# Preln attention and FFN kernel: the first head's keys by matmul instead of by copies, tables sent earlier, two V batches moved

## The chip, the cores and the metric

One core of one Trainium2 chip runs the kernel. The metric is the device time of one execution in microseconds (us). Of that, the profile shows the span, from the first to the last instruction. Engines are named as in the profile: PE is TensorE's matmul, PEld its weight load, DVE VectorE, ACT ScalarE, POOL GpSimd, SP SyncE; a q behind a name is the engine's sequencer.

## The reference

x has 4 batches of 1024 tokens of 128 features. One layer of attention and one linear layer, both on a layer norm without weights, both added to x:

```python
x = L0_attn_x                                   # (4, 1024, 128)
x = x + _L0_attn_ref(_layernorm(x), w_in, w_gate, b_gate, amplitudes, sharpness, offsets)
x = x + _L0_ffn_ref(_layernorm(x), weight, bias)

def _L0_attn_ref(x, ...):                       # H = 16 heads of HD = 8
    k, v, q = jnp.split(x @ w_in, 3, axis=-1)   # then heads()
    scores = jnp.einsum('bhqd,bhkd->bhqk', q, k) * scale + _tisa_bias(...)[None]
    attn = jnp.einsum('bhqk,bhkd->bhqd', jax.nn.softmax(scores, axis=-1), v)
    a, g = jnp.split(out @ w_gate + b_gate, 2, axis=-1)
    return a * jax.nn.sigmoid(g)
```

`_tisa_bias` is, per head, a sum of 21 Gaussians of the distance between key and query. The linear layer rounds its input and weight to FP8.

## The kernel before

**Three blocks.** `attention_block` is written as blocks of five instruction streams, one for each engine; a block ends when all engines have drained, and then the next begins. The first block (line 301 on) prepares: statistics and layer norm of x, projections, bias tables, a bound on the scores, and the data of head 0. The second (L688) does work only if the bound says that a maximum must be subtracted (`flag` is 1), which it doesn't here; but each of SP, PE and DVE loads the flag from SBUF into a register at the end of the first block and branches on it in the second. The third has the loop over eight pairs of heads and then the gate and the FFN.

**First block.** For each batch b of 1024 tokens PE transposes the normed rows (`turn`), and makes Q, K and V (`q_of`, `k_of`, `v_of`) into PSUM banks 2 and 3, 4 and 5, 6 and 7. ACT takes the high f16 half of Q and K out of PSUM into `split` (parts 0 and 2: `q_high`, `k_high`), DVE the low half, the difference (parts 1 and 3: `q_low`, `k_low`). Features lie on partitions, so `split[0:8]` is head 0. V goes to `v_all`, evacuated by ACT for batches 0, 2, 3 and by DVE for batch 1. `bias_vectors` sums the Gaussians into bank 6, from where ACT copies `gvh` and `gv` (`bias_copies`, semaphore `gh_ready`) and DVE the rest `gvl` and its maximum (`gl_ready`). GpSimd squares Q and K for the bound, ACT the keys of the last two batches (`k_square`); PE sums squares by head (`norms`), DVE takes the maxima, PE turns them twice, and a chain of tiny DVE instructions ends in `flag`.

**Data of a head.** The loop reads `qb` (queries) and `kb` (keys) with 64-row halves, in each of which `qb` holds the high and the low queries twice (rows 0 to 15 and 16 to 31), `kb` the high key twice (from rows 0 and 8) and the low key twice (from rows 16 and 24), and row 32 is -1 in `kb` against the maximum in `qb`. For heads 1 to 15 SP loads these rows from `q_scratch` and `k_scratch`, where `store_qk` wrote them (L260, L263: four stores of 256 KB a batch). For head 0 the queries are made by PE with a choice matrix `pick` (`first_queries`) and copied by ACT out of banks 4 and 5. Its keys are copied by SP within SBUF, eight rows at a time (`load_keys`, L298, 16 transfers), and their -1 rows are filled by DVE at the start. The biases come from three tables in DRAM, `g_dram`, `gh_dram` and `gl_dram` (written at L333, leading dimension 4 in the destination), loaded as overlapping slices (`load_bias`, `load_bias_parts`: 960 KB and twice 248 KB, L234, L237, L238).

**Order on SP.** All of the transfers named stand in one program order on SP: stores of batches 0 and 1; the high keys of batches 0 to 2; stores of batch 2; the low keys of 0 to 2; the tables; high keys of batch 3; a wait for the tables to land; the loads of head 0's biases; low keys of batch 3; the load of `flag` (L344). In the third block SP waits for the copies of keys (`first_in`), credits `head_in[0]`, and stores batch 3.

**The loop.** Three of the four batches of a group go PE scores, DVE adds the bias (L973), ACT exponential (L1007); for the fourth PE adds the bias itself (L923) and ACT takes it from PSUM (L1015). PE then multiplies by V (L939), two groups behind the scores (`LAG`). The first scores wait for `head_in[0]`.

## Time and profile before

| | |
|---|---|
| median of 3 runs | 611.16 us (610.3 to 612.54) |
| profiled execution | 611.27 us, span 609.5 us |
| PE busy | 566.5 us, 93% of the span |
| DVE busy | 550.2 us, 90% |
| ACT busy | 547.9 us, 90% |
| POOL busy | 72.8 us, 12% |

The page begins with busy times, then cuts the span into 40 slices of some 15 us. Then come the DMA queues, the chain of work that ended last (each piece is followed back to what released it), and the costliest groups of instructions. The chain, asked for a stretch, is listed in order of time. A stretch can also be asked for its instructions in order, for the waits in it, and for its busy times with granted clock and DMA rate.

### The profile page before, as it was taken

Reading aid. Unit: us, or ns where it says so; the run is one execution under the profiler, and the core shown is the slowest. Engines: PE = TensorE matmul, PEld = TensorE weight load, DVE = VectorE, ACT = ScalarE, POOL = GpSimd, SP = SyncE. Lnnn points to the kernel's source line nnn. Section 1 sums busy time; section 2 is a strip of 40 time slices with the busy share of each in tenths; the row PEclk is TensorE's granted clock in tenths of the full one; section 3 lists DMA queues with packets and bytes.
Section 4 is the critical chain, followed back from the end, with each engine's and each line's share of the span. In section 5 each row is a group of like instructions: output and inputs, shape, how many; then the busy total and the mean of one; then the engine's idle time right before and its main releaser. Section 6 shows DMA issues by size and latency. Waiting matters only on the chain.

```text
span 609.5 us, 12631 instructions
## 1 busy us (share of the span) xinstructions
PE 566.5 (93%) x4054; PEld 157.7 (26%) x4054; DVE 550.2 (90%) x666; ACT 547.9 (90%) x607; POOL 72.8 (12%) x85
## 2 busy tenths in 40 slices
PE   9980899999999999999999999999999999999645
PEld 4650122222222222222222222222222222227522
DVE  8960899999999999999999999999999999975885
ACT  6860899999999999999999999999999999993555
POOL 5360400000100010001000100010001000001730
PEclk9996699999999999999999999999999999999858
DMA  7344513132413241324132413241325031500004
GB/s 186 139 101 137 178 45 114 39 100 72 123 45 102 70 129 38 105 67 125 42 112 59 130 37 112 59 131 37 116 55 137 30 120 52 135 3 1 1 1 138
DMA packets 29263, 52.13 MB, mean 86 GB/s; under 512 B 9301, under 2 KB 20606, under 8 KB 28286
## 3 DMA queue, kind: packets, MB, share of 16 engines
q1 hardware_dynamic: 27358, 51.40, 30.5%
q10 hardware_dynamic: 1888, 0.53, 0.4%
q8 instruction: 8, 0.13, 0.1%
q14 instruction: 9, 0.07, 0.1%
HBM read 42.13 MB, written 9.01 MB: 84 GB/s over the span
## 4 chain that ended last, share of the span: by engine, by line
ACT 41%; issue 38%; PE 8%; DVE 5%; DMA 2%; SPq 2%; POOL 1%; ACTq 1%; DVEq 0%; POOLq 0%
ACT pbuf L1007 17%; ACT split L1007 17%; ACT split L1015 3%; ACT pbuf L1015 2%; PE ps L638 2%; DMA gl_scratch<-gvl 2%; SPq L298 1%; PE ps L574 1%; PE ps L582 1%; POOL st L1161 1%; PE ps L939 1%; DVE amax L1463 1%; PE ps L914 1%; ACTq L1006 1%; DMA kb<-split 1%
## 5 line engine op out<-in xcount | busy, mean ns | idle before, releaser
L973 DVE TENSOR_TENSOR pbuf<-ps,t 128x1024 f32<-128x1024 f32 x192 | 231.1, 1220 | 19.7 <-PE ps L914 15.0
L973 DVE TENSOR_TENSOR split<-ps,t 128x1024 f32<-128x1024 f32 x192 | 233.4, 1223 | 10.3 <-PE ps L914 4.6
L1007 ACT ACTIVATE pbuf<-pbuf 128x1024 f32<-128x1024 f32 x192 | 204.0, 1252 | 15.4 <-DVE pbuf L973 15.2
L1007 ACT ACTIVATE split<-split 128x1024 f32<-128x1024 f32 x192 | 201.9, 1259 | 1.2 <-DVE split L973 1.2
L914 PE MATMUL ps<-qb,kb 33*128 33x512 f16 x1024 | 182.7, 390 | 18.3 <-SPq L843 13.9
L939 PE MATMUL ps<-pbuf,vst 128*32 128x512 f32 x1024 | 137.2, 608 | 0.0
L939 PE MATMUL ps<-split,vst 128*32 128x512 f32 x1024 | 136.0, 604 | 1.0 <-ACT split L1015 1.0
L914 PEld LDWEIGHTS ps<-qb,kb 33*128 33x128 f16 x1024 | 48.6, 93 | 303.8 <-DVE pbuf L973 110.6
L923 PE MATMUL ps<-t64s,ident 128*64 128x512 f16 x512 | 80.5, 395 | 0.0
L1015 ACT ACTIVATE split<-ps 128x1024 f32<-128x1024 f32 x64 | 78.2, 1221 | 0.0
L1015 ACT ACTIVATE pbuf<-ps 128x1024 f32<-128x1024 f32 x64 | 77.6, 1213 | 0.0
L275 POOL COPY vst<-v_all 128x256 f32 (+1 forms) x16 | 6.4, 400 | 271.9 <-PE ps L939 252.2
L888 POOL TENSOR_TENSOR o_sbs<-o_sbs,rd 128x1024 f32<-128x1024 f32 x7 | 16.7, 2386 | 176.5 <-DMA rd<-r_scratch 176.5
L939 PEld LDWEIGHTS ps<-split,vst 128*32 128x32 f32 x1024 | 20.3, 108 | 31.5 <-issue 29.7
L939 PEld LDWEIGHTS ps<-pbuf,vst 128*32 128x32 f32 x1024 | 20.2, 108 | 29.2 <-issue 29.2
L923 PEld LDWEIGHTS ps<-t64s,ident 128*64 128x64 f16 x512 | 18.1, 108 | 31.3 <-issue 31.3
L1153 POOL TENSOR_TENSOR x_sb<-x_sb,pbuf 128x256 f32<-128x256 f32 x16 | 11.5, 725 | 43.2 <-DVE pbuf L1432 43.2
L1241 PE MATMUL ps<-ident,split 128*128 128x128 f32 x32 | 7.1, 388 | 9.9 <-issue 4.9
L1199 PE MATMUL ps<-wgate,v_all 113*128 113x256 f32 x64 | 15.2, 386 | 0.8 <-DVE pbuf L1432 0.8
L1313 ACT ACTIVATE split<-x_sb,shift,st 128x128 f32<-128x128 f32 x21 | 8.5, 481 | 7.6 <-DVE shift L1453 7.6
L1306 ACT ACTIVATE pbuf<-ps 128x256 f32<-128x256 f32 x16 | 5.1, 383 | 9.6 <-PE ps L1208 9.6
L638 PE MATMUL ps<-zeros 128*128 128x512 f16 x45 | 12.4, 442 | 1.1 <-POOL zeros L350 1.1
(141 smaller groups left out, 297.8 us busy)
## 6 DMA issues: line engine op xcount, KB each, us to landing
t<-g_scratch SPq DMA_DIRECT2D x16, 960.0 KB
kb<-k_scratch SPq DMA_DIRECT2D x120, 64.0 KB
t64s<-gh_scratch SPq DMA_DIRECT2D x16, 248.0 KB
t64s<-gl_scratch SPq DMA_DIRECT2D x16, 248.0 KB
qb<-q_scratch SPq DMA_DIRECT2D x60, 64.0 KB
x_sb<-in_L_attn_x SPq DMA_DIRECT2D x4, 512.0 KB, 7.7
q_scratch<-split SPq DMA_DIRECT2D x8, 256.0 KB, 2.8
k_scratch<-split SPq DMA_DIRECT2D x8, 256.0 KB, 2.9
```

Of the source, the lines that this page charges most:

```text
L638: eng.matmul(ps[:, 7, :], zeros[:, 0:P], zeros[:, :], start=True, stop=True)
L888: eng.tensor_tensor(o_sb, o_sb, rd[:, :], ALU.mult).then_inc(o_norm, 1)
L914: last = eng.matmul(ps[:, u + c, :], kb[p][rows, keys], qb[p][rows, b * HALF:(b + 1) * HALF], start=True, stop=True)
L923: last = eng.matmul(ps[64 * m:64 * m + 64, u + c, :], ident2[:, :], t64[p][:, c0:c0 + HALF], start=False, stop=True, skip_group_check=True)
L939: last = eng.matmul(ps[32 * b:32 * b + 32, 6 + c, :], vst[p][:, b * TB + t, :], slot(g, b)[:, c * HALF:(c + 1) * HALF], start=(t == 0 and ...
L973: eng.tensor_tensor(slot(g, b), banks(unit(k), 2), t128[p][:, t * P:t * P + S], ALU.add).then_inc(z_ready, 1)
L1007: eng.activation(buf, buf, ACT.Exp).then_inc(p_ready, 1)
L1015: eng.activation(buf, banks(4, 2), ACT.Exp).then_inc(p_ready, 1)
L1153: eng.tensor_tensor(xs, xs, gate[:, j % NG, :], ALU.add).then_inc(x1_ready, 1)
L1199: eng.matmul(gate_ps(i)[:, m * 2 * D:(m + 1) * 2 * D], num[b][0:EARLY + 1, t * P:(t + 1) * P], wgate[:, :], start=(m == 0), stop=True, ski ...
L1241: last = eng.transpose(turn_ps(g)[:, m * P:(m + 1) * P], xn2[:, n, :], ident[:, :])
L1313: last = eng.activation(xn2[:, n, :], x_sb[:, tile_of(n), :], ACT.Identity, bias=shift[:, n:n + 1], scale=st[:, 0, n:n + 1])
```

## The change

Head 0's keys are made as its queries are: PE multiplies the high and low keys of a batch by `pick_k`, a choice matrix of 128 columns that puts high and low rows into both halves (`first_keys`, four matmuls a batch), and the rows of -1 come with the evacuation, which adds a column `minus_one` (0, and -1 in rows 32 and 96): on ACT by Identity with a bias for batches 0 to 2, on DVE for batch 3 (`fk_last`). The 16 copies within SBUF and the DVE fills go. GpSimd fills `pick_k` and `minus_one` and makes two more casts.

On SP the stores of batches 0 to 2 follow each other, the tables are issued behind them as soon as they are ready, then the loads, and the stores of batch 3 move from the third block's start to the end of the first, behind the loads. V of batches 2 and 3 moves to the end of the block on PE and on ACT, into banks 2 and 3 and banks 4 and 5; the first queries' PSUM moves to banks 6 and 7. Left out of the diff are tile and semaphore declarations.

```diff
@@ -279,7 +282,8 @@
         NEG1_PAIR = float(np.array([-1.0, -1.0], np.float16).view(np.float32)[0])
-        FIRST = 3
+        FIRST = 4
+        SECOND = FIRST + 2
@@ -291,12 +295,13 @@
...
-        def load_keys(eng, part, rows, t):
-
-            for c in range(2):
-                for r in rows:
-                    eng.dma_start(kb[0][ROW * c + r:ROW * c + r + HD, t], split[0:HD, part, t]).then_inc(first_in, 16)
-        MOST, LAST = slice(0, (B - 1) * S), cols(B - 1)
+        def v_ps(b):
+
+            return banks((6, 6, 2, 4)[b], 2)
+
+        def key_ps(b):
+
+            return banks((6, 4, 2, 4)[b], 2)
@@ -321,23 +326,16 @@
...
-                store_qk(eng, 0, qk_out)
-                store_qk(eng, 1, qk_out)
-                eng.wait_ge(kh_ready, B - 1)
-                load_keys(eng, 2, (0, 8), MOST)
-                store_qk(eng, 2, qk_out)
-                load_keys(eng, 3, (16, 24), MOST)
+                for b in range(B - 1):
+                    store_qk(eng, b, qk_out)
                 eng.wait_ge(gh_ready, 2)
...
                     eng.dma_start(dst.rearrange("h (c n) -> c h n", n=HALF), src[:, :]).then_inc(g_out, 16)
-                eng.wait_ge(kh_ready, B)
-                load_keys(eng, 2, (0, 8), LAST)
                 eng.wait_ge(g_out, 16 * 3)
...
                 load_bias_parts(eng, 0, 0, head_in[0])
-                eng.wait_ge(kl_ready, B)
-                load_keys(eng, 3, (16, 24), LAST)
+                store_qk(eng, B - 1, qk_out)
                 eng.wait_ge(consts_in, 16 * 9)
@@ -352,7 +350,9 @@
...
                 eng.memset(ones_row[:, :], 1.0).then_inc(filled, 1)
+                eng.memset(minus_one[:, :], 0.0).then_inc(filled, 1)
                 eng.memset(pick[:, :, :], 0.0).then_inc(pick_ready, 1)
+                eng.memset(pick_k[:, :, :], 0.0).then_inc(pick_ready, 1)
                 for n, (dst, value) in enumerate(value_fills(0)):
@@ -373,6 +373,10 @@
...
                 eng.wait_ge(filled, FIRST)
+                eng.wait_ge(values_filled, 2)
+                eng.memset(minus_one[32:33, :], -1.0).then_inc(filled, 1)
+                eng.memset(minus_one[96:97, :], -1.0).then_inc(filled, 1)
+                eng.wait_ge(filled, SECOND)
                 eng.sem_inc(groups_done, SETS)
@@ -380,11 +384,16 @@
...
                 inverse_std(0)
-                eng.wait_ge(pick_ready, 1)
+                eng.wait_ge(pick_ready, 2)
                 eng.wait_ge(ident_in, 16)
+                unit8 = ident[:, 0:HD]
                 for i in range(2):
                     for r in (0, 16):
-                        eng.tensor_copy(pick[:, i, r + HD * i:r + HD * i + HD], ident[:, 0:HD]).then_inc(pick_ready, 1)
+                        eng.tensor_copy(pick[:, i, r + HD * i:r + HD * i + HD], unit8).then_inc(pick_ready, 1)
+                for i in range(2):
+                    eng.tensor_copy(pick_k[:, i, :].rearrange("p (c r d) -> p c r d", c=2, d=HD)[:, :, 2 * i:2 * i + 2, :],
+                                    bass.AP(tensor=unit8.tensor, offset=unit8.offset,
+                                            ap=[list(unit8.ap[0]), [0, 2], [0, 2], [1, HD]])).then_inc(pick_ready, 1)
                 for b in range(1, B):
@@ -435,7 +444,7 @@
...
                     eng.wait_ge(v_ready, b + 1)
-                    eng.activation(v_all[:, tiles(b), :].rearrange("p n d -> p (n d)"), banks(6, 2), ACT.Copy)\
+                    eng.activation(v_all[:, tiles(b), :].rearrange("p n d -> p (n d)"), v_ps(b), ACT.Copy)\
                        .then_inc(v_copied, 1)
@@ -449,15 +458,20 @@
...
                     eng.wait_ge(fq_ps, b + 1)
-                    eng.activation(qb[0][:, b * HALF:(b + 1) * HALF], ps[:, 4 + b % 2, :], ACT.Copy)\
+                    eng.activation(qb[0][:, b * HALF:(b + 1) * HALF], ps[:, 6 + b % 2, :], ACT.Copy)\
                        .then_inc(fq_ready, 1)
+
+                def first_keys(b):
+                    eng.wait_ge(fk_ps, b + 1)
+                    eng.activation(kb[0][:, cols(b)], key_ps(b), ACT.Identity, bias=minus_one[:, 0:1])\
+                       .then_inc(fk_ready, 1)
...
                                 (turn, 2), (gaussian, 2), (q_high, 2), (k_high, 2), (turn, 3), (k_square, 2),
-                                (bias_copies, 0), (q_high, 3), (k_high, 3), (k_square, 3), (v_copy, 2),
-                                (first_queries, 0), (first_queries, 1), (v_copy, 3), (first_queries, 2),
-                                (first_queries, 3)):
+                                (bias_copies, 0), (q_high, 3), (k_high, 3), (k_square, 3), (first_keys, 0),
+                                (first_keys, 1), (first_queries, 0), (first_queries, 1), (first_keys, 2),
+                                (first_queries, 2), (first_queries, 3), (v_copy, 2), (v_copy, 3)):
                     step(n)
@@ -492,8 +506,6 @@
...
-                for dst, value in minus_rows(0):
-                    eng.memset(dst, value).then_inc(kb_filled, 1)
                 stats_of(0)
@@ -549,6 +561,9 @@
...
                 eng.tensor_scalar(flag[:, :], small[0:1, 3:4], -1.0, 1.0, ALU.mult, ALU.add).then_inc(flag_ready, 1)
+                eng.wait_ge(fk_ps, B)
+                eng.tensor_scalar(kb[0][:, cols(B - 1)], key_ps(B - 1), minus_one[:, 0:1], None, ALU.add)\
+                   .then_inc(fk_last, 1)
                 eng.wait_ge(flag_ready, 1)
@@ -585,13 +600,14 @@
...
                     eng.wait_ge(xT_ready, b + 1)
-                    if b >= 1:
-                        eng.wait_ge(v_copied, b)
+                    if b == 1:
+                        eng.wait_ge(v_copied, 1)
                     if b == 2:
-                        eng.wait_ge(gh_ready, 2)
-                        eng.wait_ge(gl_ready, 2)
+                        eng.wait_ge(fk_ready, B - 1)
+                    if b == 3:
+                        eng.wait_ge(fk_last, 1)
                     for n in range(TB):
-                        last = eng.matmul(banks(6, 2)[:, n * P:(n + 1) * P],
+                        last = eng.matmul(v_ps(b)[:, n * P:(n + 1) * P],
                                           xT[:, b * S + n * P:b * S + (n + 1) * P], win[:, D:2 * D],
@@ -611,16 +627,34 @@
...
                     if b == 0:
-                        eng.wait_ge(pick_ready, 5)
-                        eng.wait_ge(kl_ready, B)
+                        eng.wait_ge(ql_ready, B)
+                        eng.wait_ge(fk_ready, 1)
                     elif b >= 2:
...
                         for i in range(2):
-                            last = eng.matmul(ps[64 * c:64 * c + 64, 4 + b % 2, :], pick[:, i, :], split[:, i, t],
+                            last = eng.matmul(ps[64 * c:64 * c + 64, 6 + b % 2, :], pick[:, i, :], split[:, i, t],
                                               start=(i == 0), stop=(i == 1))
                     last.then_inc(fq_ps, 1)
+
+                def first_keys(b):
+
+                    if b == 0:
+                        eng.wait_ge(pick_ready, 8)
+                        eng.wait_ge(kl_ready, 1)
+                        eng.wait_ge(gh_ready, 2)
+                        eng.wait_ge(gl_ready, 2)
+                    if b == 1:
+                        eng.wait_ge(kl_ready, B)
+                    if b == 3:
+                        eng.wait_ge(fk_ready, 2)
+                    for c in range(2):
+                        t = slice(b * S + c * HALF, b * S + (c + 1) * HALF)
+                        for i in range(2):
+                            last = eng.matmul(key_ps(b)[:, c * HALF:(c + 1) * HALF], pick_k[:, i, :], split[:, 2 + i, t],
+                                              start=(i == 0), stop=(i == 1))
+                    last.then_inc(fk_ps, 1)
@@ -654,22 +688,26 @@
...
                 k_of(3)
-                v_of(2)
+                first_keys(0)
                 eng.wait_ge(hsel_ready, 1)
...
                 norms(1)
+                first_keys(1)
                 first_queries(0)
                 first_queries(1)
-                v_of(3)
                 eng.wait_ge(bnd_ready, 1)
                 eng.transpose(ps[0:3, 0, 0:P], bnd[:, 0:3], ident[:, :]).then_inc(bndT_ready, 1)
+                first_keys(2)
                 eng.wait_ge(bndr_ready, 1)
                 eng.transpose(ps[0:1, 0, 256:259], bndr[0:3, :], ident[0:3, 0:3]).then_inc(bndt_ready, 1)
+                first_keys(3)
                 first_queries(2)
                 first_queries(3)
+                v_of(2)
+                v_of(3)
                 eng.wait_ge(flag_ready, 1)
@@ -690,11 +728,8 @@
...
-                    eng.wait_ge(first_in, 16 * 16)
                     eng.wait_ge(head_in[0], 16 * (LOADS - QK_LOADS - 2))
-                    store_qk(eng, B - 1, g_again)
-                    eng.wait_ge(qk_out, 16 * 4 * (B - 1))
-                    eng.wait_ge(g_again, 16 * 4)
+                    eng.wait_ge(qk_out, 16 * 4 * B)
                     with eng.Fori(0, H) as h:
@@ -839,11 +874,8 @@
...
-                eng.wait_ge(first_in, 16 * 16)
                 eng.sem_inc(head_in[0], 16 * (QK_LOADS + 2))
-
-                store_qk(eng, B - 1, qk_out)
-                eng.wait_ge(filled, FIRST + LATER)
+                eng.wait_ge(filled, SECOND + LATER)
                 eng.sem_inc(queue_steps, 1)
@@ -870,14 +902,13 @@
...
-                eng.wait_ge(kb_filled, 2)
                 eng.wait_ge(values_filled, 2)
...
                 for n, (dst, value) in enumerate(later_fills):
-                    eng.wait_ge(filled, FIRST + n)
+                    eng.wait_ge(filled, SECOND + n)
                     eng.memset(dst, value).then_inc(filled, 1)
-                eng.wait_ge(filled, FIRST + LATER)
+                eng.wait_ge(filled, SECOND + LATER)
                 eng.sem_inc(queue_steps, 1)
```

## Rows read from the trace of the kernel before

**Rows 1.** The profile page: span, and the granted clock in 40 slices.
```profile
span 609.5 us, 12631 instructions
...
PEclk9996699999999999999999999999999999999858
```

**Rows 2.** Chain of waits, 0 to 75 us: start, us, what.
```profile
42.46 10.24 DMA gl_scratch<-gvl
...
56.46 3.83 DMA kb<-split
...
60.38 0.63 PE ps L914 x2
```

**Rows 3.** PE's instructions in order: start, us, engine, line, operation.
```profile
13.13 1.24 PE L638 MATMUL ps<-zeros 128*128 128x512 f16 x5
...
38.47 1.95 PE L594 MATMUL ps<-win,pbuf 128*128 128x128 f32 x16
...
45.40 1.06 PE L621 MATMUL ps<-split,pick 128*64 128x512 f16 x8
...
68.90 1.93 PE L939 MATMUL ps<-pbuf,vst 128*32 128x512 f32 x8
...
77.22 1.06 PE L939 MATMUL ps<-split,vst 128*32 128x512 f32 x8
```

**Rows 4.** DVE's instructions in order, the same columns.
```profile
36.18 0.69 DVE L529 TENSOR_TENSOR gvl<-ps,gvh 128x512 f16<-128x512 f32 x1 [2.93 <-ACT gv L448]
...
42.62 1.21 DVE L538 TENSOR_REDUCE bnd<-ps 128x1 f32<-128x1024 f32 x1
...
46.48 0.14 DVE L551 TENSOR_SCALAR flag<-small 1x1 int32<-1x1 f32 x1
...
77.42 7.50 DVE L973 TENSOR_TENSOR pbuf<-ps,t 128x1024 f32<-128x1024 f32 x6
```

**Rows 5.** SP's issues in order, the same columns.
```profile
35.86 1.29 SPq L260 DMA_DIRECT2D q_scratch<-split  x1
37.19 0.60 SPq L263 DMA_DIRECT2D k_scratch<-split  x1
37.83 2.78 SPq L298 DMA_DIRECT2D kb<-split  x4
40.73 0.61 SPq L333 DMA_DIRECT2D g_scratch<-gv  x1
...
52.72 0.34 SPq L234 DMA_DIRECT2D t<-g_scratch  x1
...
54.35 2.74 SPq L298 DMA_DIRECT2D kb<-split  x4
```

**Rows 6.** Stretches: us, busy by engine, PEclk, DMA share, GB/s; DMA landings.
```profile
40.50:42.50 2.00, 1.68 (x24) 0.76 (x24) 1.47 (x2) 1.23 (x3) 0.17 (x1) 1.00 0.54 52
47.50:50.00 2.50, 0.00 (x0) 0.00 (x0) 0.00 (x0) 0.00 (x0) 0.00 (x0) 1.00 0.48 109
50.00:50.50 0.50, 0.00 (x0) 0.00 (x0) 0.00 (x0) 0.00 (x0) 0.00 (x0) 0.76 0.24 82
70.50:71.00 0.50, 0.50 (x6) 0.10 (x2) 0.00 (x0) 0.50 (x2) 0.00 (x0) 0.76 1.06 415
...
q_scratch<-split SPq DMA_DIRECT2D x8, 256.0 KB, 2.8
```

**Rows 7.** Waits and drains where the first (L301) and second block (L688) end.
```profile
L301 SPq DRAIN  x1: 13/13/13, 58.6 to 58.6; - x1
...
L688 PEldq EVENT_SEMAPHORE  x1: 51/51/51, 59.7 to 59.7; - x1
```

**Rows 8.** The tile flag: durations in ns, least, median, most; first and last start.
```profile
L674 PEldq TENSOR_LOAD <-flag x1: 2322/2322/2322, 46.7 to 46.7; - x1
L344 SPq TENSOR_LOAD <-flag x1: 977/977/977, 57.2 to 57.2; - x1
```

**Rows 9.** ACT's instructions in order.
```profile
39.73 1.06 ACT L443 ACTIVATE pbuf<-split 128x1024 bf16<-128x1024 f16 x1
```

More of the change, by code:

```diff
@@ L139, in attention_block @@
         pick = sb("pick", [P, 2, 64], F16)
+        pick_k = sb("pick_k", [P, 2, P], F16)
+        minus_one = sb("minus_one", [P, 1], F32)
         hselb = sb("hselb", [P, 32], BF16)
@@ L199, in attention_block @@
         hsel_ready = sem("hsel_ready")
-        kb_filled = sem("kb_filled")
         values_filled = sem("values_filled")
@@ L204, in attention_block @@
         fq_ready = sem("fq_ready")
+        fk_ps = sem("fk_ps")
+        fk_ready = sem("fk_ready")
+        fk_last = sem("fk_last")
         wq_ready = sem("wq_ready")
@@ L208, in attention_block @@
         head_in = [sem(f"head_in{p}") for p in range(2)]
-        first_in = sem("first_in")
         vst_in = sem("vst_in")
@@ L713, in _ @@
                     load_maxima(eng, 0, 0, g_again)
-                    eng.wait_ge(g_again, 16 * (4 + LOADS_G + 2))
+                    eng.wait_ge(g_again, 16 * (LOADS_G + 2))
                     eng.sem_inc(g_steps, 1)
```

## The prediction

> **What bounds the kernel now.** I read the page first. TensorE, VectorE and ScalarE are each busy for nine tenths of nearly every slice of a span of 609.5 us; the exceptions are the opening slices and the last ones, and the line of the granted clock shows one early pair of slices at 0.6 [rows 1]. So the opening is the place where a change of this kind can act, and I read the chain of waits there. It leaves the engines at the fourth round of the projections and then runs through SP: copies of keys, the three tables written to DRAM, then 10.24 us in which nothing but the landing of the last table is waited for, then the loads back, then again copies of keys, whose last one lands 3.83 us after its issue. SP's wait for it, at the head of the third block, lets the first matmul of the head loop start at 60.38 [rows 2]. TensorE has had nothing to do since 46.46 [rows 3], so 13.9 us of idle time stand between the preparation and the loop, and everything after 60.38 follows at the loop's own pace (3.75 us for a group of three adds of VectorE, 7.50 us for six [rows 4]). The term that I need is therefore the new time of that first matmul.
>
> Three things lie under the 13.9 us, and the change touches all: the way of the tables (SP's issues [rows 5]), the copies of keys on the same queue, and the crossing from the first block to the third, which needs every engine at its end.
>
> **The tables.** SP issues the copies of part 3 of three batches at 37.83 and takes 2.78 us for it, and the first table only at 40.73 [rows 5]. Its data were ready when VectorE ended the subtraction that writes gvl, at 36.18 + 0.69 = 36.87 [rows 4]. In the new order batch 2's stores stand ahead of the tables without copies between them; their last input is made by k_low(2), which VectorE does before that subtraction, and four stores cost 0.60 to 1.29 us each to issue [rows 5], so SP is free well before 36.87. The first table goes out at 36.9, 3.8 us sooner.
>
> From the first table's issue to the landing of the last it now takes 52.70 - 40.73 = 12.0 us [rows 2, 5]. In 40.5 to 42.5 the queue moved 52 GB/s at half of the 16 engines' time, which is the copies of keys, each eight rows; when only tables and short copies were left it moved 109 GB/s at 0.48 [rows 6]. At 109 GB/s the 512 KB of the three tables need 4.7 us. Around it stand some 2 us from issue to landing (a store of 256 KB on an idle queue lands after 2.8 us [rows 6], its own bytes among them), so the floor is 6.7 us; the ceiling is the 12.0 us of today. I take 9: at least the 1.8 us from 40.73 to 42.5, in which keys moved and the first table waited behind them, go, and about 1.2 us of the copies queued on the same engines later; the rest of the tables' own slowness I leave. So the tables are in DRAM at about 46.0 (43.6 to 48.9) instead of 52.7.
>
> The Trainium skill (DMA: Bandwidth & Descriptors, section "Why a DMA increments its semaphore by 16 and not by 1") says that a transfer whose outermost dimension has size 4 runs on four of the sixteen engines; the tables' destination is arranged that way. The 109 GB/s above agree with few engines. The page's fixed 2 us and its rate per engine would put the landing near the floor, 43.6; by the next paragraphs that would not move the end, since other things are later by then.
>
> **The loads and the last store on SP.** Loads of head 0 are issued from 52.72 [rows 5] and the loop's first matmul starts 7.66 us later; this is an upper bound of their own time, since the copies of keys are served between them. From 46.0 it gives 53.6 at most. Behind the loads now stand the four stores of batch 3 instead of four copies of keys (2.74 us of issue [rows 5]). By 0.60 to 1.29 each they take 2.4 to 5.2; I take 3.1. SP: 46.0 + 1.6 (52.72 to 54.35) + 3.1 = 50.7. From its last issue (57.09) to its drain at the block's end 1.5 us pass, 0.98 of them the load of the flag into a register [rows 7, 8]. SP is done at 52.2. The stores don't have to land before the loop: the waits on them stand at its third group.
>
> **TensorE, ScalarE and VectorE in the first block.** Here the change adds work where idle time was. A 128x512 f16 matmul costs 1.24 / 5 = 0.25 us [rows 3], so a batch of keys (four) costs 0.9 to 1.0 us on TensorE; the evacuation is that of k_square's size, 1.06 us [rows 9], on ScalarE, and one on VectorE. I followed the new program order with those durations. TensorE: keys 0 at 38.5 take the place of V batch 2; norms, as now, until 41.9; keys 1 until 42.8; queries 0 and 1 until 43.8; the maxima are ready when VectorE ends its second reduction at 42.62 + 1.21 = 43.83 [rows 4]; keys 2 until 45.0, keys 3 until 46.1, queries 2 and 3 until 47.1. Then V batch 2 (its banks need keys 2 evacuated, at 46.1) and V batch 3, at 1.8 us each (1.95 for the sixteen, their tail overlapped [rows 3]): 48.9 and 50.7. ScalarE evacuates V until 51.8. VectorE does the flag as now, 46.62 [rows 4], then the last keys until 47.9; V batch 3 waits for that, queued on TensorE, and would otherwise start at 48.9, so this added wait costs nothing. What stands behind V batch 3 on TensorE does cost: the load of the flag, 2.32 us [rows 8], which now runs beside nothing. If TensorE's sequencer has passed its matmuls on by about 50.0, its drain is at 52.7. The earliest this could be is 50.3 (load beside the matmuls), the latest 53.4 (load only after the last of them).
>
> **The crossing.** Today SP's drain at 58.55 is followed by TensorE's last block semaphore at 59.7 and, with the last transfer in, by the matmul at 60.38 [rows 7, 2]; without that transfer it would have started at about 59.8. So 1.25 us after the last drain. New start: 52.7 + 1.25 = 54.0, the tables' landing at 53.6 just under it. The gain is 60.38 - 54.0 = 6.4 us.
>
> **Edits at nothing.** The two fills of VectorE at the start, 3.5 us, lay ahead of statistics that wait for x in any case; the new fills and two casts on GpSimd fall into its pauses before the inverse deviations; the keys' rows of -1 come with the bias. If GpSimd's squares came later than 40.7 through them, norms and all behind would shift by as much, but they start only when VectorE's last normalisation is done. The later head loads move with the loop.
>
> **The clock.** It fell to 1.2 GHz in 50.0 to 50.5, 3.8 us after TensorE's last matmul, and came back in 70.5 to 71.0 [rows 6], 10.4 us after the loop's first matmul. Meanwhile eight product matmuls took 1.93 us for 1.06 [rows 3], so each microsecond of products at the low clock loses about half of itself; products began at 68.90, hence the loss today is 0.9 us, and perhaps 0.3 in the first scores. The new pause of TensorE runs from 50.7 to 54.0, 3.3 us. I keep today's loss in the forecast, as the middle between a clock that stays (1.2 us better) and one that comes back later against the loop's start (each 3 us later costs 1.5 us).
>
> **Sum.** The profiled execution took 611.27 us for its span of 609.5, and stands 0.1 above the median of 611.16. 611.27 - 6.4 = 604.9 us.
>
> **Rivals.**
> (a) The clock stays high across the short pause. For it: 3.3 us is under the 3.8 after which it fell. Against: the clock also fell late in the kernel with matmuls still scattered about. 604.9 - 1.2 = 603.7 us.
> (b) The tables are as slow without the keys: 12 us from 36.9, so 48.9; loads in by 56.5, first matmul then. For it: the low rate went on after the copies had ended. 611.27 - 3.9 = 607.4 us.
> (c) The end of the first block becomes the bound by more than I reckon: V batches, their copies and the flag's load in a row on TensorE, all at their upper ends, or a table load on ScalarE for the Identity function (no row shows Identity beside Exp). First matmul at 56 to 56.5: 606.9 to 607.4 us. The same time as (b), told apart by who drains last.
> (d) The change does not carry through to the end: the loop starts earlier, but its third group or the second head waits for the stores and loads, which now contend: 609 to 612 us. Against: measured from the loop's start, the stores go out 6 us earlier than now.
> (e) Slower. The low stretch was 20 us long (50.3 to 70.8 at most [rows 6]), half of it over before the loop began. Should it begin at about 60, the whole stretch would lie on products from 62.5 on: 18 us of them lose 9 to 10 us, and 604.9 + 9.5 = 614.4. It decides from a fall later than 5 us after the loop's start, with no earlier return. Against it: from the first products at 68.90 the clock needed only 1.9 us to return.
>
> **How the numbers follow.** The forecast, 604.9 with 604.2 to 606.2 as its own range: 0.40. (a) 0.25, (b) 0.10, (c) 0.13, (d) 0.08, (e) 0.04. A range of 602.6 to 607.9 holds the forecast, (a), (b), (c) and leaves the rest out. About 0.5% (3 us) is what a measurement of this kernel can tell from no change: the bound is 608.1 and 614.2. Faster 0.89, same 0.08, slower 0.03.
>
> **What would show it.** The tables' first issue near 36.9; its issue-to-landing near 9 us; a drain of TensorE or SP near 52 to 53; the first score matmul at 54; group pace 3.75 unchanged; the clock's fall after 52 or not at all. It is wrong if the tables land after 49, if ScalarE or TensorE drain after 54, or if the loop's start moved by 6 us and the end did not.

## The result, and the profile after

The changed kernel takes 606.2 us (median of 6 runs, 604.52 to 607.89) against 611.3 us for the kernel before (6 runs beside it, 610.3 to 612.54): a ratio of 0.9909, 95% interval 0.9889 to 0.993. The profiled execution took 606.47 us, span 604.7. The forecast was 604.9 us with a range of 602.6 to 607.9; its own narrower range ended at 606.2, where the result lies.

The page of the changed kernel, as [rows 1] of before:

```profile
span 604.7 us, 12656 instructions
...
PEclk9998799999999999999999999999999999999958
```

The reader should see a span 4.8 us shorter, and that the dip of the clock in the fourth and fifth slice is smaller, not gone. The chain of waits of the changed kernel (start, us, what), against [rows 2]:

```profile
54.21 0.88 SPq L877
55.09 0.05 issue
55.13 0.41 PE ps L945 x2
```

The line at L877 is SP's credit to `head_in[0]` at the head of the third block. TensorE waits beyond it for the last landing of the loads, which comes at 55.09 (the 0.88 us are that wait). The first score matmul starts at 55.13 where it was 60.38, 5.25 us earlier; the span is shorter by 4.8, so about 0.45 us are lost behind the start. SP's issues, against [rows 5]:

```profile
37.49 0.67 SPq L334 DMA_DIRECT2D g_scratch<-gv  x1
38.20 0.59 SPq L334 DMA_DIRECT2D gh_scratch<-gvh  x1
38.83 0.55 SPq L334 DMA_DIRECT2D gl_scratch<-gvl  x1
46.66 0.34 SPq L237 DMA_DIRECT2D t<-g_scratch  x1
...
50.25 0.77 SPq L266 DMA_DIRECT2D k_scratch<-split  x1
```

VectorE's and TensorE's instructions in order, against [rows 4] and [rows 3]:

```profile
36.71 0.69 DVE L541 TENSOR_TENSOR gvl<-ps,gvh 128x512 f16<-128x512 f32 x1 [2.93 <-ACT gv L457]
...
47.54 3.84 PE L610 MATMUL ps<-win,pbuf 128*128 128x128 f32 x32
55.13 0.60 PE L945 MATMUL ps<-qb,kb 33*128 33x512 f16 x4 [3.75 <-SPq L877]
...
63.43 1.93 PE L970 MATMUL ps<-pbuf,vst 128*32 128x512 f32 x8
...
68.67 1.06 PE L970 MATMUL ps<-pbuf,vst 128*32 128x512 f32 x8
...
72.60 2.45 DVE L1004 TENSOR_TENSOR pbuf<-ps,t 128x1024 f32<-128x1024 f32 x2
```

And the drains at the first block's end, against [rows 7] (ns; start):

```profile
L306 DVEq DRAIN  x1: 271/271/271, 47.8 to 47.8; - x1
L306 PEldq DRAIN  x1: 872/872/872, 50.6 to 50.6; - x1
L306 ACTq DRAIN  x1: 1054/1054/1054, 51.4 to 51.4; - x1
L306 SPq DRAIN  x1: 13/13/13, 53.0 to 53.0; - x1
```

Put beside the steps of the forecast (us from the span's start):

| | before | forecast | after |
|---|---|---|---|
| gvl written | 36.87 | 36.9 | 37.40 |
| first table issued | 40.73 | 36.9 | 37.49 |
| tables in DRAM, loads issued | 52.72 | 46.0 | 46.66 |
| TensorE's drain done | 49.4 | 52.7 | 51.4 |
| ScalarE's drain done | 47.2 | 51.8 | 52.5 |
| SP's drain | 58.55 | 52.2 | 53.05 |
| loads issued to first matmul | 7.66 | 7.6 at most | 8.47 |
| first score matmul | 60.38 | 54.0 | 55.13 |
| from it to the fifth group's first add | 17.04 | as before | 17.47 |

Half a microsecond of the difference to the forecast is this execution's own: all of its projections run 0.5 us later than in the trace of before, up to the maxima. In another profiled execution of the same kernel (the first experiment) gvl is written at 36.84 and the loop starts at 54.52.

### The profile page after: what moved, and what is told of

The parts are those of the page before. It is cut to its first block, busy times and chain, and to the rows that moved or that the text cites. A ratio compares the mean times of both kernels' runs of the same rounds, so it can differ in the third digit from the quotient of the medians.

```text
span 604.7 us, 12656 instructions
## 1 busy us (share of the span) xinstructions
PE 570.6 (94%) x4070; PEld 158.9 (26%) x4070; DVE 547.9 (91%) x665; ACT 551.0 (91%) x610; POOL 73.5 (12%) x91
## 4 chain that ended last, share of the span: by engine, by line
ACT 41%; issue 38%; DVE 5%; PE 3%; POOL 1%; ACTq 1%; SPq 0%; DVEq 0%
ACT split L1038 17%; ACT pbuf L1038 17%; ACT split L1046 3%; ACT pbuf L1046 2%; PE ps L970 1%; POOL st L1192 1%; DVE amax L1494 1%; PE ps L945 1%; ACTq L1037 1%; DVE split L1487 1%; DVE pbuf L1463 1%; DVE stats L1472 0%; PE ps L1230 0%; DVE pbuf L1004 0%; ACT kb L1381 0%
## 5 line engine op out<-in xcount | busy, mean ns | idle before, releaser
L919 POOL TENSOR_TENSOR o_sbs<-o_sbs,rd 128x1024 f32<-128x1024 f32 x7 | 16.7, 2385 | 174.6 <-DMA rd<-r_scratch 174.6
L954 PEld LDWEIGHTS ps<-t64s,ident 128*64 128x64 f16 x512 | 18.1, 108 | 31.3 <-issue 31.3
```

The lines of the kernel that those rows point to most:

```text
L919: eng.tensor_tensor(o_sb, o_sb, rd[:, :], ALU.mult).then_inc(o_norm, 1)
L954: last = eng.matmul(ps[64 * m:64 * m + 64, u + c, :], ident2[:, :], t64[p][:, c0:c0 + HALF], start=False, stop=True, skip_group_check=True)
```

## The experiments

Each was timed against the kernel before on the same chip, but the chip is not the same for all: one for `again` to `warm_fill`, one for `keys_on_queue` to `v_in_halves_warm`, one for the last two. Across these groups the ratios are to be compared, not the medians. In the table the start is the profiled execution's first score matmul; the tables' time goes from the first store's issue to the first load's; "landed" is the last landing of the three loads (each of the engines that carried a part posts one, 48 in all); groups 0 to 3 go from the start to the fifth group's first add.

| kernel | ratio to before (95%) | median us | tables | loads, issue to landed | start | groups 0 to 3 |
|---|---|---|---|---|---|---|
| before | 1 | 611.3 | 12.0 | 52.72 to 60.24 | 60.38 | 17.0 |
| again (the changed kernel) | 0.9908 (0.9894 to 0.9922) | 606.12 | 9.1 | 46.06 to 54.48 | 54.52 | 17.2 |
| stores_back | 0.9909 (0.9895 to 0.9924) | 606.17 | 9.15 | 46.05 to 54.24 | 54.29 | 18.1 |
| tables_by_quarter | 0.9884 (0.9869 to 0.99) | 604.71 | 6.6 | 43.50 to 51.01 | 53.05 | 17.7 |
| warm_fill | 0.9912 (0.9891 to 0.9934) | 605.48 | 9.1 | 46.13 to 54.75 | 54.82 | 16.1 |
| keys_on_queue | 0.9988 (0.9977 to 1.0) | 610.72 | 11.2 | 51.84 to 59.32 | 59.37 | 18.2 |
| tables_before_low_keys | 0.9961 (0.9948 to 0.9974) | 608.75 | 11.75 | 49.53 to 56.76 | 57.39 | 17.7 |
| v_in_halves | 0.9878 (0.9863 to 0.9892) | 603.63 | 6.6 | 43.62 to 51.02 | 52.75 | 16.7 |
| v_in_halves_warm | 0.9895 (0.988 to 0.9909) | 604.92 | 6.6 | 43.51 to 50.86 | 54.03 | 16.1 |
| v_in_halves_light | 0.989 (0.9861 to 0.9918) | 604.13 | 6.6 | 43.72 to 51.05 | 52.85 | 15.3 |
| before_by_quarter | 0.9984 (0.9974 to 0.9994) | 610.22 | 10.2 | 50.92 to 58.40 | 58.78 | 17.2 |

**The changed kernel again**, without an edit.

> The changed kernel as it is, as the yardstick of this group. Ratio to the kernel before 0.991 (0.989 to 0.993). Loop start (first score matmul) near 55, some 5 us earlier than in the kernel before.

0.9908: the result stands in five more executions. Its trace is the one to compare the next three with, since its projections end as early as theirs.

**Were the moved stores what slowed the loads?** The four stores of batch 3 go back to the start of the third block:

```diff
                 load_bias_parts(eng, 0, 0, head_in[0])
-                store_qk(eng, B - 1, qk_out)
                 eng.wait_ge(consts_in, 16 * 9)
...
                 eng.sem_inc(head_in[0], 16 * (QK_LOADS + 2))
+                store_qk(eng, B - 1, qk_out)
                 eng.wait_ge(filled, SECOND + LATER)
```

> The changed kernel with batch 3's four stores back at the start of the third block, nothing behind the loads of head 0's biases in the first. In the changed kernel those loads took 8.4 us from first issue to the last landing (46.66 to 55.09), and the loop started with that landing. Theory A (the stores moved behind the loads share the queue with them and delay their last landing): the loads take 7.5 us or less again, the loop starts 0.9 us or more earlier relative to the issue of the loads, with SP's drain near 50.5; the bound is then ScalarE's drain (52.4) plus the crossing, first matmul near 53.7; 1.0 to 1.4 us faster than the changed kernel. Rival B (the late landing has another cause, for instance an instruction fetch on one DMA engine): the loads still take 8.4 us and the time stays within 0.4 us of the changed kernel's.

Rival B holds: the loads take 8.2 us without anything behind them, the loop waits for them 1.21 us after SP's credit, and the time is the same. (The loop starts 0.2 us earlier than in `again`, and groups 0 to 3 take 0.9 longer: in this execution the clock was already low from 53.4, and until 67.0.) What holds the last landing up shows in the DMA view of this kernel from 51.6 to 53.2 us (40 slices: share in tenths, then GB/s; then the queues with packets, MB and share of 16 engines):

```profile
DMA  0949400040000000000000000000000000060000
GB/s 0 199 99 410 99 0 0 0 99 0 0 0 0 0 0 0 0 0 0 0 0 0 0 0 0 0 0 0 0 0 0 0 0 0 0 99 0 0 0 0
...
q1 hardware_dynamic: 13, 0.02, 7.9%
q8 instruction: 1, 0.02, 5.1%
```

For more than 1 us fifteen engines are idle and the loads are not complete. The only thing in flight is one packet of the instruction queue, a fetch of 16 KB: 5.1% of 16 engines over 1.6 us is 1.3 us of one engine. The last three packets of the loads, 3968 bytes each, follow one another from 53.02, when it ends. The landings say the same: 47 of the loads' 48 are in by 52.84, the last comes at 54.24; in the changed kernel 53.93 and 55.09, in `again` 53.43 and 54.48. Over the loads' whole time the same view has the line in three kernels, first the changed kernel (46.6 to 55.0), then `again` (46.0 to 54.4), then `stores_back` (46.0 to 54.2):

```profile
q8 instruction: 1, 0.02, 0.7%
```
```profile
q8 instruction: 1, 0.02, 0.9%
```
```profile
q8 instruction: 1, 0.02, 1.0%
```

`warm_fill` has it too (0.7% from 46.1 to 54.7). The other kernels have such a fetch too, but not in the loads' way. In `tables_by_quarter` and the three built on it, it starts at 50.9 to 51.3, and the loads' last packets end at 50.2 to 50.6; the kernel before has it at 42.98 and `keys_on_queue` at 47.17, ahead of the loads. With the fetch ahead of their last packets the loads take 8.2 to 8.6 us, in all other kernels 7.2 to 7.5; where the stores stand makes 0.2 (8.4 in `again`, 8.2 here). That the fetch delays the landing is shown by the hole above and by this grouping. So the change seems not to have added a fetch but to have made one come 9 us later; what sets its moment was not tried.

**Why do 512 KB of tables take 9 us?**

```diff
                 for src, dst in ((gv, g_dram), (gvh, gh_dram), (gvl, gl_dram)):
-                    eng.dma_start(dst.rearrange("h (c n) -> c h n", n=HALF), src[:, :]).then_inc(g_out, 16)
-                eng.wait_ge(g_out, 16 * 3)
+                    for c in range(4):
+                        eng.dma_start(dst[:, c * HALF:(c + 1) * HALF], src[32 * c:32 * c + 32, :]).then_inc(g_out, 16)
+                eng.wait_ge(g_out, 16 * 12)
```

> The changed kernel with each table written by four transfers of 32 rows each instead of one whose destination's outermost dimension is 4. Theory A (the table stores are slow, 9.15 us from first issue to last landing for 512 KB, because each runs on few DMA engines; 109 to 125 GB/s): twelve issues of 0.35 to 0.6 us take 5 to 7 us, the last lands about 2 us behind, so 7 to 8.5 us in all: loads go out 0.7 to 2 us earlier, and the loop starts earlier by up to 1 us, no more, as ScalarE's drain at 52.4 plus the crossing comes next. Rival B (the rate is set by descriptors or by DRAM writes, not by the number of engines): the stores take 9 to 11 us, and the time is the same or up to 2 us worse.

Theory A, and better than its own bounds: 6.6 us instead of 9.1. The trace also counts the engines. The semaphore of the tables is updated 15 times in the changed kernel, once about 1 us behind its issue and then by four landings for each of the three stores, and here 192 times, 16 for each of the twelve. SP's issues in this kernel:

```profile
36.87 1.74 SPq L335 DMA_DIRECT2D g_scratch<-gv  x4
38.65 1.83 SPq L335 DMA_DIRECT2D gh_scratch<-gvh  x4
40.52 1.81 SPq L335 DMA_DIRECT2D gl_scratch<-gvl  x4
43.50 0.36 SPq L237 DMA_DIRECT2D t<-g_scratch  x1
```

Twelve issues take 5.5 us and the last of them is in DRAM 1.2 us later: the stores are now bound by their issue. Of the 2.6 us gained there only 1.5 reach the start, as the loads' landing at 51.0 is no longer the last: ScalarE's drain is.

```profile
L306 SPq DRAIN  x1: 7/7/7, 49.9 to 49.9; - x1
L306 PEldq DRAIN  x1: 552/552/552, 50.2 to 50.2; - x1
L306 ACTq DRAIN  x1: 1052/1052/1052, 50.8 to 50.8; - x1
```

It ends at 51.85 and the first matmul stands 1.2 us behind it, which confirms the 1.25 us of the crossing. So the two V copies, moved to the block's end, are the next bound. The move costs nothing while the tables are slow; no run has the V batches back in their old places.

**What does the clock cost at the start?** Matmuls of zeros, results not used:

```diff
                 v_of(3)
+                for _ in range(5):
+                    eng.matmul(ps[:, 1, :], zeros[:, 0:P], zeros[:, :], start=True, stop=True)
...
+                fill(4)
                 for g in range(LAG):
                     for b in range(B):
                         scores(0, g, b)
+                        fill(2)
```

> The changed kernel with matmuls of zeros added on TensorE: five behind V batch 3 in the first block, four ahead of the first scores, and two behind each of the eight score steps ahead of the loop (25 in all, results not used). In the changed kernel the granted clock fell to 1.2 GHz at 56.5 and came back at 66.7, with products from 63.4. Theory A (the idle stretches around the loop's start cost the clock, and the clock costs half of each microsecond of products under it): the clock stays at 2.4 GHz through 50 to 70, the first four groups take 15.0 to 15.6 us instead of 16.9, the kernel is 1.3 to 1.9 us faster than the changed kernel. Rival B (the start is bound by VectorE's adds and DMA, the clock costs nothing there): no change, or up to 1 us slower by the added matmuls.

The clock stayed at 2.4 GHz, and groups 0 to 3 took 16.1 us instead of 17.2 (17.5 in the first profile of the changed kernel). Theory A is right on the clock and wrong on the time: the start came 0.3 later, the median is 0.6 us under that of `again` but the ratio is 0.9912 against 0.9908, so no gain is shown. Two of the six executions took 608.02 and 608.57 us, with a mean clock of 0.976 where the other four have 0.979 to 0.982. The fillers have a price of their own: between the groups VectorE waits 0.59 us for the scores, against 0.16 with one filler behind each step instead of two (the light filling below). The price of the low clock shows in the stretch of the changed kernel in which products ran under it: eight of them took 1.93 us at 63.43 and 1.06 at 68.67.

**Is it the copies on the queue, or the order of issue?** The eight copies of batches 0 to 2 are put back where they were, into rows of the second head's tile that nothing reads at that time; the keys still come from TensorE:

```diff
-                for b in range(B - 1):
-                    store_qk(eng, b, qk_out)
+                store_qk(eng, 0, qk_out)
+                store_qk(eng, 1, qk_out)
+                eng.wait_ge(kh_ready, B - 1)
+                copy_keys(eng, 2, (0, 8))
+                store_qk(eng, 2, qk_out)
+                copy_keys(eng, 3, (16, 24))
```

> The changed kernel with the eight copies of three batches' keys put back on SP's queue where the kernel before had them, ahead of batch 2's stores and ahead of the tables, into a tile that is not read (the keys of head 0 are still made by TensorE). Theory A (these copies, by their issue and by the time they hold the DMA engines on which the tables queue, are what the change took out of the tables' way): the first table is issued at 40.5 to 41 instead of 37.2 and the tables take 11 to 12 us instead of 9.2, loads go out near 52, the loop starts near 60: 5 us slower than the changed kernel, about the kernel before. Rival B (the tables are slow for their own sake, only the issue order counts): issue at 40.7 but landing 9.2 us behind it, loop start near 58, 3.5 us slower than the changed kernel.

Theory A: the tables go out at 40.63 and need 11.2 us, the loop starts at 59.37, and by the ratios (0.9988 against 0.9908) some 4.9 of the changed kernel's 5.6 us are gone, though 8 of the 16 copies are still missing. Of the 4.85 us by which the start is later, the issue order accounts for 3.7 (40.63 against 36.92), the copies' hold on the engines for 2.1 (11.2 against 9.1); the loads, with no instruction fetch among them, give 0.9 back (7.5 against 8.4). SP's issues there:

```profile
37.73 2.78 SPq L304 DMA_DIRECT2D kb<-split  x4
40.63 0.66 SPq L347 DMA_DIRECT2D g_scratch<-gv  x1
...
51.84 0.34 SPq L237 DMA_DIRECT2D t<-g_scratch  x1
```

**How much would the order alone have given?** The kernel before, with one move:

```diff
                 store_qk(eng, 2, qk_out)
-                load_keys(eng, 3, (16, 24), MOST)
                 eng.wait_ge(gh_ready, 2)
...
                     eng.dma_start(dst.rearrange("h (c n) -> c h n", n=HALF), src[:, :]).then_inc(g_out, 16)
+                load_keys(eng, 3, (16, 24), MOST)
```

> The kernel before with one move: the three tables are issued ahead of the copies of the low keys of batches 0 to 2 instead of behind them. Theory A (what counts is what stands ahead of the tables): the first table goes out near 38 instead of 40.7 and lands up to 2.5 us sooner, but the low keys now stand behind the tables on the same few engines and are needed before the loop; gain 1 to 3 us of the 5.4. Rival B (the copies must land before the loop in any order, and are the bound with the tables early): no gain, within 0.5 us of the kernel before.

2.4 us faster by the ratio (0.9961), inside theory A's 1 to 3. The tables go out 3 us earlier, at 37.78, but still take 11.75 us to the first load, since SP itself issues keys in between: the last table landed at 47.86, SP reached the loads at 49.53. The last of the copies, not the tables, is what the loop then waits for:

```profile
40.28 9.21 SPq L298 DMA_DIRECT2D kb<-split  x8
49.53 0.44 SPq L234 DMA_DIRECT2D t<-g_scratch  x1
```
```profile
53.37 3.94 DMA kb<-split
57.34 0.05 issue
57.39 0.63 PE ps L914 x2
```

The first lines are SP's issues, the second the chain of waits. Eight issues take 9.21 us, over 1 us each, where the four of 51.25 take 0.69 each; a queue that is full would do that, but no run tests it.

**The same quartering on the kernel before** (the edit of tables by quarter, there alone).

> The kernel before with each table written by four transfers of 32 rows, nothing else. Theory A (the tables' 12.0 us were the copies ahead of them on the queue and the few engines of each store, and each counts by itself): the tables take 8 to 9.5 us, the loop starts 2.5 to 4 us earlier. Rival B (the copies ahead set the landing, whatever the stores' form): within 1 us of the kernel before.

Neither theory whole: the last table landed 8.65 us after the first issue, as A said, but the start moved by 1.6 us only. The time moved by 1 (0.9984), at the edge of what B said, but not for B's reason. SP needs 7.4 us to issue the twelve behind the copies and 2.66 for four more copies, so that the loads wait for SP until 50.92, not for the tables:

```profile
40.67 3.79 SPq L334 DMA_DIRECT2D g_scratch<-gv  x4
...
48.22 2.66 SPq L298 DMA_DIRECT2D kb<-split  x4
50.92 0.44 SPq L234 DMA_DIRECT2D t<-g_scratch  x1
```

Of the 3.3 us by which the last table landed sooner, 1.8 reached the loads. The same edit is worth 0.0024 of the time on the changed kernel and 0.0016 here, and 1.5 and 1.6 us of the start; the intervals don't tell the two apart.

**The next bound, ScalarE's copy of V.** Tables by quarter, and V batch 3 in halves:

```diff
                     for n in range(TB):
                         last = eng.matmul(v_ps(b)[:, n * P:(n + 1) * P], ...)
+                        if b == 3 and n == TB // 2 - 1:
+                            last.then_inc(v_ready, 1)
...
+                def v_half(i):
+                    eng.wait_ge(v_ready, 4 + i)
+                    n0 = 3 * TB + i * (TB // 2)
+                    eng.activation(v_all[:, n0:n0 + TB // 2, :].rearrange("p n d -> p (n d)"), ps[:, 4 + i, :],
+                                   ACT.Copy).then_inc(v_copied, 1)
```

> Tables by quarter (each table in four transfers) and, besides, V batch 3 handed to ScalarE in two halves of four tiles, so that the first is copied while TensorE makes the second. In tables by quarter the last to end in the first block was ScalarE, drain done at 51.85, and the first score matmul stood 1.2 us behind, at 53.05, with the loads landed at 51.0. Theory A (the block's end, now ScalarE's copy of V, is the bound): ScalarE is done 0.5 us sooner, the loop starts at about 52.5, 0.5 us faster than tables by quarter. Rival B (the crossing or another engine is the bound at the same time): no change.

Theory A's way, at somewhat more than half its size: ScalarE's drain ends at 51.54 instead of 51.85, the loop starts at 52.75 instead of 53.05. The ratios differ by 0.0006, 0.4 us, and their intervals overlap. The profiled executions are 1.2 us apart: 0.3 of this is the start, the rest lies in the first groups (16.7 against 17.7), where this execution's clock was low for 6.8 us (from 55.9 to 62.7), against 10.2 in the profile of tables by quarter. By its median this is the fastest of all versions, 603.63 us, 7.9 us under the kernel before beside it.

**Both gains together, with heavy and with light filling.** First the whole filling of the warm kernel on V in halves:

> The kernel of the previous run with the matmuls of zeros of the warm filling (five, four, and two behind each of eight score steps). Alone on the changed kernel these kept the clock at 2.4 GHz around the loop's start and brought the fourth group 1.1 us forward, but the loop's start went back by 0.3 and the median gained 0.6 only. Theory A (the two gains add): 0.5 to 1 us faster than without the filling, the clock high from 15 to 575. Rival B (the filling pays for itself only when the start is late, or brings another slow stretch in some executions, as two of its six runs at 608 suggest): median equal to or above that without it, wider spread.

Rival B: 604.92, not better than without, and by the medians 1.3 us slower (the wider spread that B named did not come, the four lie within 0.7 us). The chain of waits shows why:

```profile
53.07 1.02 PE ps L991 x4
54.10 0.32 PE ps L956 x2
54.42 0.54 PE ps L991 x2
```

The four fillers ahead of the scores (L991), hidden in the changed kernel while TensorE waited for the loads, now delay them by 1.02 us, and the five behind V delay TensorE's drain to 51.86. Then three behind V, none ahead of the scores, one behind each step:

```diff
                         scores(0, g, b)
+                        eng.matmul(ps[:, 7, :], zeros[:, 0:P], zeros[:, :], start=True, stop=True)
```

> V in halves (which has tables by quarter) with fewer matmuls of zeros: three behind V batch 3, none ahead of the first scores, one behind each of the eight score steps. With five, four and sixteen of them the loop started 1.3 us later than in V in halves and the clock stayed at 2.4 GHz. Theory A (the four ahead of the scores and the five ahead of TensorE's drain stood in the way of the start, the rest only fills pauses): start within 0.2 us of V in halves, clock not below 2.4 GHz from 15 to 575, fourth group 16.0 us behind the start instead of 16.7, and 0.3 to 0.7 us faster. Rival B (so few don't hold the clock): the clock falls as in V in halves, and the time is the same.

The profiled execution did what theory A said, and more: start 52.85, the clock high until 566, waits of only 0.16 us between the adds of groups 0 to 3, groups in 15.3 us, 602.69 us.

```profile
53.38 3.48 DVE L1016 TENSOR_TENSOR pbuf<-ps,t 128x1024 f32<-128x1024 f32 x3 [5.80 <-PE ps L956]
57.02 3.48 DVE L1016 TENSOR_TENSOR pbuf<-ps,t 128x1024 f32<-128x1024 f32 x3 [0.16 <-PE ps L956]
60.67 7.50 DVE L1016 TENSOR_TENSOR split<-ps,t 128x1024 f32<-128x1024 f32 x6 [0.16 <-PE ps L956]
```

But its six executions are 602.24, 602.36, 602.69, 605.57, 605.67 and 607.62 us, with mean granted clocks of 0.98, 0.98, 0.977, 0.973, 0.972 and 0.968. Between the ends 0.012 of the clock is some 14 us more at the low level in a span of 600 (at half the full clock a mean lower by 0.012 is 0.024 of the span), and the times differ by 5.4 us. The kernel with the filling is not better by its median. Whether the long ones had the clock down in the first groups, so that the filling failed to hold it, or at the kernel's end is not settled, as only one execution of each kernel leaves a trace; that the clock made the 5.4 us is argued from the means alone.

## Why the prediction was right, point by point

The mechanism was right: the tables' way was the bound, and what stood ahead of them on SP's queue and on the engines made them late. The size was less well met. 5.1 us were gained where 6.4 were forecast, and by time alone 606.2 lies nearer to the 606.9 of rival (c) than to 604.9; the trace tells them apart.

**The tables' start: right.** They go out 0.1 us behind the subtraction of gvl, as read from [rows 4], in every kernel without copies ahead of them.

**The tables' time: right.** 9 us were taken between 6.7 and 12.0; 9.2 and 9.1 measured. Of the 12.0 us, `keys_on_queue` ascribes about 2.1 to the eight copies ahead. Another 0.8 is the difference between that kernel's 11.2 and the 12.0 of before, which has more copies behind the tables; no run has these alone. The two together are nearly the 3 us that the prediction took off. Of the 9.1 that are left, 2.6 are the form of the stores: quartered, they take 6.6 us, at which their issue is the bound. That this is near the floor of 6.7 is chance, as the floor was reckoned for stores at 109 GB/s. The Trainium skill (DMA: Bandwidth & Descriptors, section "Why a DMA increments its semaphore by 16 and not by 1") lets a transfer whose outermost dimension is 4 run on four engines, and this case agrees: each of the three stores posts four landings, each of the twelve 16, and the same bytes in transfers with 32 rows outermost took 2.6 us less. The landing near 43.6 that the prediction worked out with the page's figures did not come; the tables were in DRAM at 46.64, and at 46.05 in `again`.

**The loads: the step that failed.** The prediction took 7.66 us as an upper bound, because the copies of keys were served between the loads in the trace of before. It was none: 8.4 to 8.5 us measured, with an instruction fetch of 1.0 to 1.3 us on one engine ahead of the last packets. In the trace of before none fell between the loads' packets (the last ends at 59.14, two fetches of 8 KB start at 59.91 and 60.04), and with stores behind the loads instead of copies, and no fetch, they take 7.3 to 7.5 against 7.5, so the copies of keys had cost them next to nothing. The term was short by 0.8, and it decided the start: the crossing alone would have allowed 54.3 in the first profile (53.05 + 1.25), the landing made it 55.13.

**The first block's end: right on the whole, with TensorE's part wrong.** SP at 53.05 and ScalarE at 52.5, with this execution's 0.5 us of delay taken off, are within 0.4 of the 52.2 and 51.8 expected. For SP that is partly luck: the four stores took 2.7 us instead of 3.1, the load of the flag 1.55 instead of 0.98. TensorE was expected last, at 52.7, because its flag load of 2.32 us would stand behind V (the earliest drain that it names, 50.3, lies ahead of its own end of V, 50.7). The load took 0.94 us and lay beside the matmuls; the drain was over at 51.4. The same load takes between 0.49 and 2.33 us in these traces, so a single row was a weak base. Rival (c) did not happen: no table load on ScalarE appeared for Identity, and the copies of keys with a bias took 1.10 us each.

**The clock: right that nothing would be gained, for an inexact reason.** I kept the loss as it was. It fell later (56.5 instead of 50.3) and came back sooner against the span (66.7 instead of 70.7), but 11.6 us behind the loop's start instead of 10.4. Products ran under it for 3.3 us instead of 1.85; at half of each microsecond that is 0.7 us more, enough for the 0.45 us more in groups 0 to 3. Rival (a), the clock that stays, did not come by itself. `warm_fill` shows 1.1 us for it in these groups, against the 1.2 priced, with 25 fillers in the way; with the light filling they took 15.3 us, 1.9 less than in `again`, so the clock at the start may be worth more than the prediction priced. The windows of the changed kernel (us, busy time by engine, PEclk, DMA share, GB/s):

```profile
56.00:56.50 0.50, 0.00 (x0) 0.00 (x0) 0.50 (x1) 0.00 (x0) 0.49 (x1) 1.00 0.22 57
56.50:57.00 0.50, 0.06 (x2) 0.06 (x4) 0.50 (x2) 0.08 (x1) 0.45 (x1) 0.51 0.07 25
66.50:67.00 0.50, 0.50 (x8) 0.00 (x0) 0.50 (x1) 0.00 (x0) 0.00 (x0) 0.75 1.05 286
```

**The other rivals.** (b), slow tables without the keys, is out: 9.1 us. (d), a gain that is given back later, is out beyond the 0.45 us: the span is shorter by 4.8, the start by 5.25. (e), a long low stretch under the products, did not decide this kernel. It was priced at 9 to 10 us for 18 us of products under the low clock; the nearest that the runs have are the light filling's six executions, in which some 14 us more of low clock go with 5.4 us.

**The sum.** 6.4 us forecast for the start; 5.25 and, in the execution whose projections ended as in before, 5.86 measured. Of the missing 0.5 to 1.1 us the fetch holds 0.8 at most and the rest is the delay of one execution against another. Groups 0 to 3 add 0.2 to 0.45 us. Together that is most of the 1.3 us between 604.9 and 606.2.

## What to carry to other kernels

When all engines pause for a chain of transfers, read what stands ahead of them on the issuing queue and on how many DMA engines each store runs; small copies within SBUF ahead of them cost twice here, by their issue (3.7 us) and by their hold on the engines (2.1 us), and matmuls with a choice matrix on an idle TensorE (1.0 us a batch) replace them for little. Count what comes last after the gain: here the way by ScalarE's drain lay 1.4 us under that by the loads, so that 2.6 us won on the stores gave 1.5. Fillers that keep the clock up delayed the start where no pause hid them, and must be judged over many executions.

## What the runs showed of the hardware that was not expected

An instruction fetch of 16 KB held one DMA engine for 1.0 to 1.3 us, and loads whose last packets came behind it took some 0.8 us longer; in `stores_back` the other fifteen engines stood idle meanwhile. Loading one value from SBUF into an engine's register took 0.49 to 2.33 us for the same instruction in different kernels. And three tables in twelve transfers of 32 rows took 6.6 us, as three of 128 rows with the outermost dimension 4 they took 9.1, although the twelve cost SP nine more issues of 0.46 us.
